# Copying attention 2's key parts into place in two column halves

## What is computed

```python
def layer0(x, context, mask):           # 16 heads of 16 channels
    Q, K, V = x @ Wq.T + bq, context @ Wk.T + bk, context @ Wv.T + bv
    s = where(mask == 0, -1e9, Q @ K.T / sqrt(16))
    return layernorm(softmax(s) @ V @ Wo.T + bo + x) * ln_g + ln_b

def layer1(x, context, pad_mask):       # 8 heads of 32 channels
    h = mamba2_block(x)                 # rms norm, in-projection, convolution, scan, gated norm, out-projection
    Q, K, V = layernorm(h) @ Wq, context @ Wk, context @ Wv
    s = where(pad_mask, -1e9, Q @ K.T / sqrt(32))
    return h + softmax(s) @ V @ Wo
```

## Time and profile before

| | us |
|---|---|
| median of 3 runs | 8695.27 |
| lowest, highest | 8695.15, 8697.0 |
| the profiled execution | 8695.25 |
| its span, first to last instruction | 8693.3 |

### The profile page before, as it was taken

How to read it: one execution, slowest core, us unless ns; L and a number is a source line. 1 busy time by engine, 2 the same in 40 slices (tenths; PEclk the granted TensorE clock), 3 DMA queues, 4 the chain that set the end, 5 groups by cost and what they waited for, 6 DMA issues and landing times.

```text
span 8693.3 us, 128104 instructions
## 1 busy us (share of the span) xinstructions
PE 7601.7 (87%) x37572; PEld 3396.5 (39%) x37572; DVE 4991.8 (57%) x12397; ACT 3399.7 (39%) x4278; POOL 1907.4 (22%) x1864
## 2 busy tenths in 40 slices
PE   3989889898998989889898898989989899898988
PEld 0343433434334343433434334343343433434343
DVE  3566465664656556465664656646566564656646
ACT  0424435243352434435244352433524335252443
POOL 3040130402203031130401304023030311303113
PEclk6989999899998989989899898999989999898998
DMA  3142240423314132131422304233141331314223
GB/s 72 26 79 37 39 69 10 79 37 50 57 21 75 30 61 55 21 69 27 76 40 36 67 14 79 37 47 60 20 76 30 56 58 19 71 30 71 45 36 61
DMA packets 216827, 422.15 MB, mean 49 GB/s; under 512 B 35673, under 2 KB 126715, under 8 KB 215945
## 3 DMA queue, kind: packets, MB, share of 16 engines
q1 hardware_dynamic: 214103, 413.20, 27.9%
q10 hardware_dynamic: 2048, 0.53, 0.0%
HBM read 191.17 MB, written 8.54 MB: 23 GB/s over the span
## 4 chain that ended last, share of the span: by engine, by line
PE 69%; DVE 11%; issue 8%; DMA 6%; ACT 3%; POOL 1%; SPq 1%; DVEq 0%; ACTq 0%; POOLq 0%
PE ps L1029 14%; PE ps L966 11%; PE ps L1000 8%; PE ps L1002 8%; PE ps L928 7%; DVE mx L1635 6%; PE ps L1004 4%; DMA kst<-khl 4%; PE ps L1034 4%; PE ps L1148 2%; PE ps L985 2%; PE ps L1239 1%; DMA qst<-q1hl 1%; PE ps L1267 1%; ACT PR L1406 1%
## 5 line engine op out<-in xcount | busy, mean ns | idle before, releaser
L1406 ACT ACTIVATE PR<-ps 128x1024 f32<-128x1024 f32 x2496 | 2499.6, 1024 | 2505.0 <-PE ps L1002 1494.4
L1606 DVE CUSTOM_DVE_ANT_0 ps<-ps,maskq 128x402 f32<-128x402 f32 x4203 | 2409.0, 587 | 1505.6 <-PE ps L966 1362.7
L1029 PE MATMUL ps<-PR,vbuf 128*32 128x512 f32 x9984 | 1343.3, 610 | 5.1 <-ACT PR L1406 5.1
L1002 PE MATMUL ps<-maskk,identb 128*128 128x512 bf16 x3328 | 1263.4, 380 | 0.0
L966 PE MATMUL ps<-kst,qst 96*128 96x402 bf16 (+1 forms) x3115 | 1019.5, 340 | 79.5 <-DVE mx L1606 64.3
L1635 DVE TENSOR_REDUCE mx<-ps 128x2 f32<-128x804 f32 x1024 | 932.6, 987 | 167.8 <-PE ps L985 164.9
L985 PE MATMUL ps<-kst,qst 100*128 100x402 f32 x2048 | 744.2, 488 | 257.8 <-DMA qst<-q1hl 155.4
L1000 PE MATMUL ps<-qst,kst 99*128 99x512 bf16 x2496 | 950.7, 381 | 0.0
L1004 PE MATMUL ps<-qst,kst 102*128 102x512 f32 x1664 | 767.9, 525 | 100.2 <-ACT PR L1406 70.8
L966 PEld LDWEIGHTS ps<-kst,qst 96*128 96x128 bf16 x3115 | 281.8, 97 | 1182.3 <-DVE mx L1606 821.3
L746 POOL MEMSET kst<- 96x252 f32 (+1 forms) x34 | 8.7, 255 | 3063.1 <-PE ps L1029 3016.6
(11 more groups left out here) (197 smaller groups left out, 7669.8 us busy)
## 6 DMA issues: line engine op xcount, KB each, us to landing
kst<-khl SPq DMA_DIRECT2D x96, 800.5 KB, 16.1
kst<-khl SPq DMA_DIRECT2D x300, 200.1 KB, 7.4
stage<-in_maskt SPq DMA_DIRECT2D x204, 256.0 KB
stage<-in_mask SPq DMA_DIRECT2D x204, 201.0 KB
ctxs<-in_ctxt SPq DMA_DIRECT2D x17, 1601.0 KB, 25.8
qst<-q1hl SPq DMA_DIRECT2D x96, 256.0 KB
win_s<-in_w_in SPq DMA_DIRECT2D x16, 1288.0 KB, 5.7
KS<-khl SPq DMA_DIRECT2D x102, 200.1 KB
```

The source lines that it names most:

```text
L1002: mm = pe.matmul(o, identb[:, :], maskk[:, t, :], start=False, stop=True)
L1029: mm = pe.matmul(ps[32 * j:32 * j + 32, 6, :], l, PR[:, t % 2, j, :], start=(t == 0), stop=(t == KT - 1), tile_position=(0, 32 * j))
L1406: nc.scalar.activation(PR[:, t % 2, 2 * half:2 * half + 2, :], ps[:, 2 * half:2 * half + 2, :], ACT.Exp, scale=scale).then_inc(s_p, 1)
L1606: nc.vector.tensor_tensor_reduce(src, src, maskq[:, i, c0:c0 + w], 1.0, -3.0e38, ALU.add, ALU.max, mx[:, c, h * QT + i:h * QT + i + 1]).th ...
```

## The change

The stacking of a key block is split at column 804, between the second and third chunk (KHALF). `stack_k1` gets a half: it waits for the second or the fourth chunk and issues three copies of that half's columns (804 or 797 of 1601), which count on a semaphore of their own, s_k1[g][half]. SP calls it for half 0 and 1 of group 0, then of group 1. ScalarE, taking chunk c of k[1], waits for the half of group 0 that holds chunk c. The other users wait for both halves. Bytes, destinations and the order of all other work stay as they are.

```diff
-        s_k1 = [sem(f"s_k1_{g}") for g in range(G1)]
+        s_k1 = [[sem(f"s_k1_{g}_{e}") for e in range(2)] for g in range(G1)]
@@
+        KHALF = [(0, KCH[NC // 2][0]), (KCH[NC // 2][0], S)]
@@
-            def stack_k1(b, g):
-                sp.wait_ge(s_restfree, rests(b, K1[NC * (g + 1) - 1]) + 1)
+            def stack_k1(b, g, half):
+
+                sp.wait_ge(s_restfree, rests(b, K1[NC * g + NC // 2 * (half + 1) - 1]) + 1)
                 alone(sp)
+                lo, hi = KHALF[half]
                 for n, (kpart, qpart) in enumerate(TERMS1):
-                    sp.dma_start(f(KS1[g][HD1 * n:HD1 * (n + 1), :, 0:S]), f(khl1[:, kpart, 0:S])).then_inc(s_k1[g], 16)
+                    sp.dma_start(f(KS1[g][HD1 * n:HD1 * (n + 1), :, lo:hi]), f(khl1[:, kpart, lo:hi]))\
+                        .then_inc(s_k1[g][half], 16)
@@
-            for first in (*s_stack, *s_mload, *s_k1, *s_qs1, *s_mload1, s_out):
+            for first in (*s_stack, *s_mload, *s_k1[0], *s_k1[1], *s_qs1, *s_mload1, s_out):
@@
                 for g in range(G1):
-                    stack_k1(b, g)
+                    for half in range(2):
+                        stack_k1(b, g, half)
@@
                 if kind == "raw" and k == 0:
-                    pe.wait_ge(s_k1[g], LEAD + (b + 1) * STACK1)
+                    for half in range(2):
+                        pe.wait_ge(s_k1[g][half], LEAD + (b + 1) * STACK1)
@@
                             for g in range(G1):
-                                act.wait_ge(s_k1[g], LEAD + b * STACK1)
+                                for half in range(2):
+                                    act.wait_ge(s_k1[g][half], LEAD + b * STACK1)
@@
                         else:
-                            act.wait_ge(s_k1[0], LEAD + (b + 1) * STACK1)
+                            act.wait_ge(s_k1[0][i[1] // (NC // 2)], LEAD + (b + 1) * STACK1)
```

## The result

| | before | after |
|---|---|---|
| median, us | 8695.21 (8693.4 to 8697.0, 4 runs) | 8574.56 (8564.75 to 8575.0, 4 runs) |
| profiled execution, us | 8695.25 | 8574.72 |
| ratio after / before | | 0.9858, 95% interval 0.9845 to 0.9872 |

The change makes the kernel 121 us faster, 7.5 us a batch. The forecast was 213 us, 13.3 a batch; its direction was right, its size and its range (8466 to 8530) were not. Of one kernel further down (fill_all) one execution of four, 9134.59 us at a mean granted clock of 0.83 against 0.96, is left out of the times.

What follows compares the result with a forecast made beforehand. The prediction took TensorE's standing behind the key stacking transfer (kst<-khl), which held up ScalarE and then POOL's aU, as the bound. 10.5 us standing plus 2.8 clock, 13.3 a batch x 16 = 213: 8695.3 - 213 = 8482 us, range 8466 to 8530.

Steps and rivals of the forecast that it cites:

- half 0 leaves earlier: Key block stacking: the first half needs K1[1] alone, so its third copy goes at 457.3 and three are landed at 468.9.
- half rows cost half: Stacking copies: bytes, not rows, set the time, so 400 KB takes 3.5 us against 7.05 for 800.5 KB.
- ScalarE's wait goes to 0: ScalarE's take of chunk 0, wanted at 475.5: its 11.26 us wait for the copies vanishes, with 6.6 us to spare.
- half 1 in time: Second half of the key block: lands at 479.5, 5.5 us before chunk 2 is in PSUM at 485.0.
- What follows in the stage: In-projection stage from window sum 3 to the last V projections: ends 13.3 us earlier a batch, 10.5 standing and 2.8 clock.
- rival A: In-projection stage: standing goes but the half clock stays from thinner work; gain 10.5 us a batch, 8527 us; chance 0.05.
- B: POOL's aU before window sum 3 waits for the whole convolution; TensorE stands 1.9 us, 8513 us; chance 0.05.
- C: Stacking copies: rows, not bytes, set the price, so both halves land late; 1.4 us a batch slower, 8718 us; chance 0.03.
- D: Stacking copies: each pays its fixed part, half 1 lands at 493.8; gain only 4.7 us a batch, 8620 us; chance 0.03.
- E: Stacking: half 0 is held by something else and ScalarE waits as now; 8695 us; chance 0.02.
- VectorE against POOL: POOL's aU beside the last convolution: VectorE ends about 481.4, hidden by 1.6 us; TensorE loses 0.1, at most 0.75 us.
- The sum: Whole kernel: 16 batches x 13.3 us = 213 us off 8695.3, giving 8482 us, 2.4% less; chance 0.80.

Runs made afterwards that it cites:

- fill_all: The change plus matmuls of constants nobody reads (fillers) in TensorE's waits from the layer norm after attention 0 through the maxima stage; 8504.27 us, ratio 0.9777.
- both_wait: The change, but ScalarE waits for both halves of group 0 before chunk 0, so only the early issue is kept; 8574.53 us (8558.93 to 8594.69).
- delay1: The change plus a GpSimd memset of about 0.5 us before the layer norm's variance in each batch, a pure delay; 8573.11 us.
- the scan's fillers: The change plus five short matmuls of constants a batch, where TensorE waits at the scan's start and for ScalarE's yt; 8585.15 us.

## Why the prediction was wrong, by its steps

- *What bounds the kernel; half 0 leaves earlier; half rows cost half; ScalarE's wait goes to 0; half 1 in time.* Right, each. The landing of half 0 is within 0.1 us; the longest landing of the copies in that stretch, 14.5 us after an issue at 462.9 at the latest, puts half 1 at 477.4 at the latest where I had 478.3 with the shift.
- *What follows in the stage*: 13.3 us a batch. Measured 13.3. So rival A (clock not given back in the stage), B (POOL), C (rows set the price), D (a fixed part for each copy) and E (the change without effect) all fell. The Trainium skill's batching rule and fit (DMA: Bandwidth & Descriptors, Bandwidth), which it gives for transfers issued from GpSimd and from which I estimated 2.5 us lost a batch in this stage, are not what the trace shows for these copies queued on SP: pieces of 400 KB landed 5.7, 8.6 and 11.3 us after issue, as bytes alone foretell. Two sums of these rivals were off by about 1 us: with 7.05 us a copy, half 1 lands at 500.8 in C (not 499.7), and at 490 by the fit (not 489). Nothing in the forecast hangs on them.
- *VectorE against POOL.* Right for TensorE: it waited for aU 8.6 / 16 = 0.5 us by the list, and in the timeline window sum 3 and its neighbour took some 0.1 to 0.2 us more than without a wait. I had 0.1 and a bound of 0.75. VectorE lost more than I had: its three taps took 4.52 us, not 3.96, and ended at 481.47, 0.3 us before ScalarE came to them and not 1.6.
- *The sum.* Here it failed. 16 x 13.3 takes the other 467 us of a batch as they were. The term for it stood in the text, "the low clock at 544 to 548 might move too, 1 us a batch either way", and was sized from that one place. It measured 5.8 us a batch: 2.5 in the scan, which the fillers show to be the clock, and 0.8, 1.7 and 0.7 after, which go with the low grant. It should have been sized from all stretches in which TensorE is thin and the grant is at either level: in the trace of before, 28 of the maxima stage's 62 us, 10 of the q1 piece's 19, and the scan with 3.48 and then 2.82 of 4 us busy, which had held the full clock and so had something to lose. What the scan could lose can be bounded from its rows before: matmuls of 0.86 to 1.1 us, which take twice as long while the grant is low.
- *The range.* Its upper end, 8530, came from clock loss inside the stage (A) and from B. A case "the grant falls in a stage that held it" was missing; with 5.8 us a batch it gives 8575.

What stays open: why the same thin work at the start of the scan kept the full grant before and lost it after. What TensorE did just ahead differs (before: standing from 480.2 to 490.7, low until 496, then 10 us of dense work; after: dense from 456 on). both_wait, with a short stall there, kept the grant in 14 of 16 batches; but delay1, without one, kept it in 7, so a stall is not needed, and small shifts in time switch the fall on and off from batch to batch. That the fall needs the thin work is shown by the scan's fillers. By what rule the chip chooses, these runs don't tell. Open too is how much of the maxima stage's 1.7 us and attention 2's 0.7 the clock accounts for: both go with the low grant from batch to batch (the two longest attention 2 pieces after, 135.9 and 136.2 us, are the two with 15.4 us of it), but no kernel with fillers reached the 62.2 and 133.4 us of before.

## What to carry to other kernels

A copy that overwrites or frees a buffer may be split where its consumer is split, with a semaphore for each piece: the first piece can leave before the producer is done, and here that, more than the finer wait, shortened the stage (10.6 of 13.3 us). When a stall goes, the granted clock of every later stage is open again: list the stages where TensorE is thin and say what each costs at either level before adding the gain up. Matmuls of constants in TensorE's waits can hold the clock and made the best version here (8481 us), but only where TensorE sets the pace and truly waits; in the maxima stage, where VectorE is nearly always busy, they cost more than they brought (8504 us against 8481).

## What was not expected of the hardware

- TensorE's grant can differ for the same work at the same density: 1.00 at 512 to 516 before, 0.71 and 0.50 at 496 to 504 after, with 3.48 and then 2.82 of 4 us busy ahead of it in both.
- The pieces of a batch take only a few values, with steps that go with the low grant: the scan 35.5 to 35.6, 36.8 to 37.05 or 38.45 us for 0, 3.4 or 6.8 us of it, in every kernel. A delay of 0.53 us in each batch changed the median by less than 2 us.
- Fillers in the waits of the kernel before moved nothing in the total (ratio 0.9999) although its in-projection stage was 4.1 us shorter and q1 1.4: 3.7 us went into the maxima stage, where some of them stood, and 1.9 into attention 2.
